# Attention and FFN on eight cores: paced first projections, the last head's bounds on TensorE, spaced small jobs, the last turn moved up

## What is computed

```python
def _layernorm(x, axis=-1, eps=1e-5): ...
# x: (4, 2048, 2048), 16 heads of 128
q, k, v = proj(q_w), proj(k_w), proj(v_w)            # of layernorm(x)
scores = einsum('bhqd,bhkd->bhqk', q, k) / sqrt(128)  # causal
av = einsum('bhqk,bhkd->bhqd', softmax(scores), v)
gate = sigmoid(einsum('bhqd,ed->bhqe', q, gate_w) + gate_b)
x = x + layernorm(concat(av * gate) @ o_w.T)
g = (layernorm(x) @ gate_w.T) * gate_s                # 5632 wide, ternary
u = (layernorm(x) @ up_w.T) * up_s
x = x + layernorm(((silu(g) * u) @ down_w.T) * down_s)
```

## Time and profile before

| | us |
|---|---|
| median of 3 runs | 1730.98 (1730.25 to 1880.8) |
| profiled execution, its own device time | 1729.22 |
| its span on the slowest core (7) | 1727.6 |
| spans of the odd cores | 1725.2 to 1727.6 |
| spans of the even cores | 1717.3 to 1719.9 |
| TensorE busy on core 7 | 1655.5 (96%) |

### The profile page before, as it was taken

The page is one execution under the profiler, slowest core; times in us unless marked ns, Lnnn a source line. Parts: engine busy times, 40 slices in busy tenths (PEclk is TensorE's granted clock), DMA queues, the critical chain, the costliest instruction groups (busy, mean ns, idle before and its releaser), DMA issues.

```text
span 1727.6 us, 29344 instructions; the slowest of 8 cores (1717.3 to 1727.6 us)
## 1 busy us (share of the span) xinstructions
PE 1655.5 (96%) x11548; PEld 1047.8 (61%) x11548; DVE 675.1 (39%) x1448; ACT 460.9 (27%) x723; POOL 127.5 (7%) x245
## 2 busy tenths in 40 slices
PE   3799999999999999998899999999999999999997
PEld 2556666666666666664445555555555557888853
DVE  5845656565555556566563111111111110121135
ACT  4744444444434444444122111111111110000012
POOL 0000000000000000000001000000000021111100
PEclk9999999999999999999999999999999999999999
DMA  9732222222231313034336545445454567555557
...
DMA packets 43921, 152.12 MB, mean 88 GB/s; under 512 B 5120, under 2 KB 6272, under 8 KB 39040
## 3 DMA queue, kind: packets, MB, share of 16 engines
...
## 4 chain that ended last, share of the span: by engine, by line
PE 87%; DVE 6%; issue 3%; ACT 3%; DVEq 0%; DMA 0%; ACTq 0%; SPq 0%
PE psum L358 86%; DVE st L388 2%; DVE psum L613 1%; PE psum L363 1%; ACT b_h1b L418 1%; ACT b_kT L475 1%; DVE b_avn L657 1%; DVE b_gat L670 0%; DVE b_xb L917 0%; DMA b_yb<-y_d 0%; ACT b_P L617 0%; DVE rc L656 0%; DVEq L1271 0%; ACT mv L371 0%; DVEq L107 0%
## 5 line engine op out<-in xcount | busy, mean ns | idle before, releaser
L358 PE MATMUL psum<-b_h2T,b_fw 128*128 128x384 bf16 (+1 forms) x2752 | 520.9, 352 | 0.0
L358 PEld LDWEIGHTS psum<-b_h2T,b_fw 128*128 128x128 bf16 x2752 | 269.3, 98 | 251.3
L358 PE MATMUL psum<-b_h1T,b_wb 128*128 128x512 bf16 (+1 forms) x1536 | 386.3, 370 | 0.4 <-DVE b_Bb L550 0.4
L617 ACT ACTIVATE b_P<-psum 128x512 bf16<-128x512 f32 (+1 forms) x368 | 218.4, 593 | 395.6 <-DVE psum L613 299.6
L613 DVE TENSOR_TENSOR psum<-psum,b_Bb 128x512 f32<-128x512 f32 (+3 forms) x512 | 251.7, 511 | 149.6 <-PE psum L358 146.1
L358 PE MATMUL psum<-b_wb,b_h1T 128*128 128x256 bf16 x2048 | 270.4, 273 | 0.0
L358 PE MATMUL psum<-b_wd,b_hdn 128*128 128x256 bf16 (+1 forms) x2156 | 268.4, 288 | 0.0
L358 PEld LDWEIGHTS psum<-b_wd,b_hdn 128*128 128x128 bf16 x2156 | 211.0, 98 | 57.2
L995 DVE SCALAR_TENSOR_TENSOR b_hdn<-psum,cf,b_sg 128x512 bf16<-128x512 f32 (+1 forms) x88 | 60.1, 684 | 465.7 <-PE psum L358 461.4
L358 PEld LDWEIGHTS psum<-b_wb,b_h1T 128*128 128x128 bf16 x2048 | 193.2, 98 | 28.5
L358 PEld LDWEIGHTS psum<-b_h1T,b_wb 128*128 128x128 bf16 x1536 | 141.6, 98 | 109.7 <-issue 0.9
...
...
## 6 DMA issues: line engine op xcount, KB each, us to landing
...
```

Of the source, the lines that this page charges most:

```text
L358: return self.q.do("T", lambda e: e.matmul(out, lhsT, rhs, start=start, stop=stop, skip_group_check=True), waits, tok)
L617: te = q.do("S", lambda e: e.activation(p[:, 0:128 * n], self.bank(b, 128 * n), ACT.Exp, scale=CSC), [ta, self.av_tok.get(gi - PRING)])
```

## The change

Parts: (1) `prologue`: `debt` is held at one `per` at most, so that a group that has become available goes out over three tiles; `gen_v` runs two tiles behind instead of one; the loop ends with the last tile and the rest of the chain follows it. V's halves are asked for with x tiles 1 and 2, K's with 3, Q's with 4 (early half) or 8 (late half), the gate's with 5 or 9. (2) Last head: no `gen_sum`, no additions on VectorE; the bound and the triangle are added by TensorE, as products with `cneg` and the identity that accumulate onto the scores; two banks instead of three. (3) `gen_o` makes both columns 1024 to 1535 (bank 6) and 1536 to 2047 (bank 7) of tile 1, 28 products, 14 in head 14 and 14 in head 15. (4) Small jobs are three half-units apart instead of two. (5) `h2_ok` is kept per tile. (6) The SiLU table is loaded before the last tile's `h2b`. (7) FFN: three blocks of the first group come early on the late half, with the turn behind the second one's products and before its SiLU. (8) A no-op on SP that waits for POOL's DMA lanes before the last tile is finished.

```diff
     def scores(self, gi, h, segs):
...
         q, r = self.q, self.r
-        b = gi % 2 if h < H - 1 else (0, 1, 6)[gi % 3]
+        b = gi % 2
         kt, qt = self.kT[h % 2], self.qT[h % 2]
         bb, bm = self.Bb[h % 2], self.Bm[h % 2]
         w = [self.tok["k_ev", h], self.tok["q_ev", h]] + self.bf[b]
...
+        if h == H - 1:
+            w += [self.tok["absq", h, i] for i in range(len(r.GROUPS))]
+            parts = []
+            for j, a, z, c in segs:
+                at = slice(128 * a, 128 * z)
+                parts.append((c, z - a, kt[:, 128 * j:128 * j + 128],
+                              qt[:, at]))
+                parts.append((c, z - a, self.k["cneg"], self.absq[:, at]))
+                if r.Q0 + a == j:
+                    parts.append((c, 1, self.k["idn"], self.k["tri"]))
+                n = c + z - a
+            for i, (c, m, lhsT, rhs) in enumerate(parts):
+                t = self.mm(self.bank(b)[:, 128 * c:128 * (c + m)], lhsT, rhs,
+                            i == 0, i == len(parts) - 1, w,
+                            tok=(i == len(parts) - 1))
+            self.tok["S_mm", h] = t
+            self.exp(gi, b, n, t)
+            return
         for i, (j, a, z, c) in enumerate(segs):
             t = self.mm(self.bank(b)[:, 128 * c:128 * (c + z - a)],
                         kt[:, 128 * j:128 * j + 128], qt[:, 128 * a:128 * z],
...
                     s, s, src[:, 128 * x:128 * y], ALU.add))(),
                     [t, self.tok["Bm", h]])
+        self.exp(gi, b, n, ta)
+
+    def exp(self, gi, b, n, ta):
...
-        te = q.do("S", lambda e: e.activation(
+        te = self.q.do("S", lambda e: e.activation(
             p[:, 0:128 * n], self.bank(b, 128 * n), ACT.Exp, scale=CSC),
             [ta, self.av_tok.get(gi - PRING)])
...
         if self.small and max(self.small[0][2], self.rested) <= self.now:
-            self.rested = self.now + 2
+            self.rested = self.now + 3
             self.small.pop(0)[3]()
...
+            if nh == H - 1:
+                continue
             if c > 0:
...
         if s == H - 2:
-            out.append(itertools.islice(self.o_part, 6))
-            cols += 512 * 6
+            out.append(itertools.islice(self.o_part, len(self.o_done)))
+            cols += 512 * len(self.o_done)
         out += sums
         if s == H - 1:
             out = [self.o_part]
-            cols = 512 * (len(self.o_done) - 6)
+            cols = 512 * len(self.o_done)
...
         for kc in self.o_done:
-            self.mm(self.bank(7)[:, :], self.gat[:, kc, 128:256],
...
-            yield 512
+            for c in (2, 3):
+                self.mm(self.bank(4 + c)[:, :], self.gat[:, kc, 128:256],
+                        self.wo_at[kc][:, 512 * c:512 * c + 512],
+                        kc == 0, False, [self.ct("wo", kc), self.gat_tok[kc]]
+                        + (self.bf[4 + c] if kc == 0 else []))
+                yield 512
...
             self.scores(gi, h, us[u])
-            goal = cols * (u + 1) / (nu if h < H - 2 else 0.92 * nu)
+            goal = cols * (u + 1) / (nu if h < H - 1 else 0.92 * nu)
...
-        for key, t in ((("v", 0, 0), 0), (("v", 0, 1), 0), (("k", 0), 1),
-                       (("q", 0), r.Q0 and 6 or 2), ("gate", r.Q0 and 7 or 4),
+        for key, t in ((("v", 0, 0), 1), (("v", 0, 1), 2), (("k", 0), 3),
+                       (("q", 0), r.Q0 and 8 or 4), ("gate", r.Q0 and 9 or 5),
...
-        for t in range(r.NK + 1):
-            if t < r.NK:
-                self.back(t)
+        for t in range(r.NK):
+            self.back(t)
...
             self.seen_tile = t - 1
-            if t < r.NK:
-                for x in self.gen_v(0, t - 1, 1):
-                    pass
+            for x in self.gen_v(0, t - 2, 1) if t > 1 else ():
+                pass
...
-            debt += per
-            while debt > 0 or t == r.NK:
+            debt = min(debt + per, per)
+            while debt > 0:
                 x = next(work, None)
                 if x is None or x == 0:
                     break
                 debt -= x
+        self.seen_tile = r.NK - 1
+        for x in work:
+            pass
+        for x in self.gen_v(0, r.NK - 2, 1):
+            pass
...
                 order = [(kc, c) for kc, c in order
-                         if c < 3 or kc not in self.o_done]
+                         if c < 2 or kc not in self.o_done]
...
+        if t == r.NQ - 1:
+            m0 = self.k["mv"][3]
+            q.do("S", lambda e: e.activation(m0[:, 7:8], m0[:, 6:7], ACT.Silu))
...
-        self.h2_ok = th
+        self.h2_ok[t] = th
...
-                             [self.h2_ok] + self.bf[b], tok=(k == 7))
+                             [self.h2_ok[t]] + self.bf[b], tok=(k == 7))
...
         self.ring, self.ring_at = [6, 7, 4, 5, 2, 3], 0
-        early = [(i, g) for i in range(2) for g in range(ng - 1)]
-        turn_at = min(len(early), 3) - 1
+        ni = 3 if ng == 2 else 2
+        early = [(i, g) for i in range(ni) for g in range(ng - 1)]
+        turn_at = len(early) - 2
+        self.cast_to("wu", 2)
         for n, (i, g) in enumerate(early):
-            self.ffn_one(i, g)
+            ready = self.ffn_mm(i, g)
             if n == turn_at:
                 self.h2_turn(r.NQ - 1)
+            self.ffn_act(i, g, ready)
         self.tok["o_rest"] = [self.h2_tr[r.NQ - 1], *self.spill.values()]
-        self.ring, self.ring_at = [0, 1, 2, 3, 4, 5, 6, 7], 2
-        self.cast_to("wu", 2)
-        for i in range(2):
+        self.ring, self.ring_at = [0, 1, 2, 3, 4, 5, 6, 7], 2 * ni
+        for i in range(ni):
             self.ffn_one(i, ng - 1)
-        self.cast_to("wu", 3)
-        for i in range(2, ITN):
+            if i == 1:
+                self.cast_to("wu", 3)
+        if ni == 3:
+            self.cast_to("wu", 4)
+        for i in range(ni, ITN):
             for g in range(ng):
                 self.ffn_one(i, g)
                 if g < 2:
...
+        q.put("Y", lambda e: e.nop(), [(s, s.val) for s in q.lanes["GD"]],
+              None, 0)
         self.finish(r.NQ - 1, tp, [512, 512, 512, 512])
```

13 lines of the change are left out of this document (9 added, 4 removed).

## The result

The changed kernel takes 1716.6 us (median of four executions, 1716.1 to 1717.7); the ratio to the kernel before is 0.992, 95% interval 0.9896 to 0.9944. That is 14.4 us less than 1731.0, and by the 2% bound no difference. I had said 1718, from 1711 to 1724. The number was nearly right, but the half that sets it was not the one I had named, and by my own last sign ("or if a core of the early half ends last") I was wrong. (In some executions the four cores of one die stood at a lower granted clock, from 0.98 down to 0.82, and took longer; they are left out, and where few are left I give the single times.)

The account below looks back on a forecast made before the run. TensorE, busy 96% of the span, was taken as the bound, with core 7 slowest. Its terms, 0 - 4.6 - 3.0 - 2.5 - 2.1 - 0.3 = -12.5, gave 1715.1 us, put on the median 1718; range 1711 to 1724.

Parts of the forecast that it names:

- my own last sign: Wrong if core 7's first scores come 3 us earlier, its last head takes 22 us, or an early-half core ends last.
- Which half ends last: Late half (core 7) still ends last, at 1715.1 us; the early half would have to gain under 3.1 us to do so.
- the weights: Start of the early half: asking for weights later gains 4 us there, ends 0 and 7.
- first projections: Start of core 7: even pace saves 4.85 us at the last turn, products moved behind it cost it back; taken as 0.
- Small jobs: First fifteen heads, core 7: three steps apart removes the wait for the gated product, -4.6 us, bounds -4.6 and 0.
- Last head: Core 7: head starts 1.0 us earlier and takes 20.2 us instead of 22.2; -3.0 us, bounds 0 and -7.
- Output projection: First turn runs at once, a wait of 5.6 us follows it; net -2.5 us at the next turn, bounds -1 and -3.4.
- Last turn and no-op: Kernel's end: a third up and gate block covers the wait behind the last turn, -2.1 us; no-op on SP, -0.3.
- (a): Rival, full cover: key maximum hides at the start and last head runs without waits; 2 + 2 us more, 1714; chance 0.15.
- (b): Rival: last head stays bound by a round trip over two banks, nothing gained there; 1722 us; chance 0.13.
- (c): Rival: the bank-5 wait in the heads moves instead of going; 1722.5 us; chance 0.12.
- (d): Rival: slower than before, added idle stretches keep TensorE at its lower clock level; 1733 us with 30 us low; chance 0.03.

Follow-up runs that it names:

- e6: The changed kernel with the old pace of the first projections (whole groups at once) and the later weights kept; one execution of 1720.0 us.
- e2: The changed kernel with the small jobs two steps apart as before; 1720.7 to 1722.6 us, ratio to the kernel before 0.9953.
- e12: The kernel before with the small jobs three steps apart instead of two, nothing else; 1724.0 to 1725.9 us, ratio 0.9969.
- e5: e4 with the last head as before the change: three score banks, its bounds added by VectorE; one execution of 1717.2 us.
- e4: The changed kernel with 14 early output products within the last two heads instead of 28; 1711.3 us, ratio to the kernel before 0.9896.

## Why the prediction was wrong, and where it was right

**Which half ends last** is the step that failed: "The early half would have to gain less than 3.1 us to end last; the weights (4) and its own output projection (2.5, by the same code) alone give more." The output projection gave its 2.5. The weights gave nothing: 4.7 us lost alone (before to e6), and made up for by the pace (e6 to changed), which I had put at 0 for core 7 and had not worked out for core 2. My reasons were that the third turn no longer stands behind the weights and that the x tiles get their bandwidth. The turn did move ahead, and it was no gain, as TensorE then waited for the weights, 5.4 us again and until 31.48 instead of 25.28. The other parts of the sum I had read on core 7 and never on an even core: its wait for `a_gat` was 0.4 us in 1, not 4.6 in 13, so spacing brings little there (it costs 0.1 by e2 and saves 1.1 by e12), and of the last head's 2.8 (e5) the fourteen added products took 2.7 back (e4). "It decides nothing while it is above -3" was wrong: with 4 us at the start the early half would have ended some 4 us earlier, below the late one. The other side of the sentence failed too. On the means of the four cores the late half led by 8.2 us (1726.6 and 1718.4); it gained 15.1 for my 12.5, and the early half 4.3 for my 6.5 and more. With 12.5 both would have ended level at 1714.1; with 15.1 the late half ends at 1711.5, and the early half decides.

**The late half** went as the sum has it, but further. By its terms: first projections 0, measured −0.2. The working behind the 0 did not hold: the loop gained 0.35 on core 7 and 2.1 on the mean, not 4.85, and what made up for it was a first turn that came 2.9 us earlier on the mean, for which no run gives a cause. That the net is 0 is luck. Small jobs −4.6, measured −7.7 (e2) and −8.3 (e12): the term was mis-sized by taking the recorded wait for its cost, 0.35 for 0.51; thirteen times 0.51 are 6.6, and the rest of the 7.7 was not followed up (of the 8.3, some is the clock's). Last head −3.0, measured −1.8 (e5, with part of it the clock's, which I had no term for); inside it, 20.2 us forecast and 20.5 measured. Output projection −2.5, measured −3.2: the wait moved behind the turn and was 4.5 us, not 5.6. Last turn and no-op together −2.4, measured −2.0, and nothing waits there. No experiment undid the third block, the table load or the no-op by itself, and the −0.3 of the no-op stood on no row; in the changed kernel the odd cores' stretch behind the last turn scatters by 2.2 us (799.4 to 801.6), so the parts can't be told apart.

**The time** came out within 1.4 us by luck: the late half gained 2.6 more than its 12.5 and fell below the early half, which gained less than I had and ends (1712.6 to 1715.9) near where I had put the late one (1715.1).

**Rivals.** (a) had the late half's surplus of 2.6 us, but not from its two places: the head took 20.5 us, not some 18, and the pace gained less, not more; the surplus is the jobs'. (b) did not occur, the head is 99% busy. (c) did not occur. (d) did not: the mean clock rose from 0.994 to 0.996 on core 7, though a lower level did follow the new stall. Its "fast again some 4.5 us later" held only for the stall in the output projection; in the last head of the kernel before the lower level lasted from 785 to past 791 us. By the Trainium skill, "TensorE: Matmul & The Clock Gate", section Seeing it yourself, a die is limited once three of its cores run dense matmuls; in the profiled executions here eight cores stand at 0.994 to 0.998, and in that of the kernel before at 0.993 to 0.996, so it did not act there.
